# A two-layer transformer kernel on one core: column sums of the softmax weights by way of GpSimd in rows 1 to 6

## The reference, cut to what matters

```python
def _L1_attn_ref(x, Wq, bq, Wk, bk, Wv, bv, Wo, bo):
    B, S, _ = x.shape                     # D_MODEL, H, DK, DV = 128, 16, 64, 64
    q = (x @ Wq + bq).reshape(B, S, H, DK)
    k = x @ Wk + bk                       # one key head for all 16 query heads
    v = x @ Wv + bv
    scores = jnp.einsum('bshd,btd->bhst', q, k) / np.sqrt(DK)
    w = jax.nn.softmax(scores, axis=-1)
    out = jnp.einsum('bhst,btd->bshd', w, v).reshape(B, S, H * DV)
    return out @ Wo + bo
```

## Time and profile before

| | |
|---|---|
| median of 3 runs | 1322.18 us (1320.48 to 1323.92) |
| the profiled execution's own time | 1316.21 us |
| its span, first to last instruction | 1314.5 us |
| TensorE busy / weight loads | 1221.6 / 724.0 us |
| VectorE (DVE) busy | 957.3 us |
| ScalarE (ACT) busy | 680.7 us |
| GpSimd (POOL) busy | 256.2 us |

### The profile page before, as it was taken

How to read it: one execution, slowest core, us unless ns; L and a number is a source line. 1 busy time by engine, 2 the same in 40 slices (tenths; PEclk the granted TensorE clock), 3 DMA queues, 4 the chain that set the end, 5 groups by cost and what they waited for, 6 DMA issues and landing times.

```text
span 1314.5 us, 21957 instructions
## 1 busy us (share of the span) xinstructions
PE 1221.6 (93%) x7185; PEld 724.0 (55%) x7185; DVE 957.3 (73%) x2332; ACT 680.7 (52%) x1252; POOL 256.2 (19%) x311
## 2 busy tenths in 40 slices
PE   5459989999999999999999999999999989998997
PEld 2335445555555555545554555465545468775743
DVE  6876788578857885788578857885787567785865
ACT  4036556544554455445544554455444467775731
POOL 2033222200120012001200120012000226262630
PEclk9559999999999999999999999999999999998999
DMA  3073667233422351334223413351333557474471
GB/s 80 0 193 86 213 195 222 64 75 84 137 57 74 81 143 54 74 87 121 70 74 88 140 51 75 82 144 51 77 85 71 165 181 243 152 240 145 136 220 55
DMA packets 100020, 150.59 MB, mean 115 GB/s; under 512 B 35341, under 2 KB 51277, under 8 KB 95941
## 3 DMA queue, kind: packets, MB, share of 16 engines
q1 hardware_dynamic: 85348, 116.59, 32.5%
q0 software_dynamic: 11344, 31.64, 7.6%
q10 hardware_dynamic: 3216, 0.97, 0.3%
HBM read 59.86 MB, written 38.68 MB: 75 GB/s over the span
## 4 chain that ended last, share of the span: by engine, by line
PE 54%; DVE 18%; issue 12%; POOL 9%; ACT 4%; DMA 2%; SPq 1%; ACTq 0%; POOLq 0%; DVEq 0%
PE bank L1500 13%; POOL y_rows L734 7%; PE bank L1472 7%; PE bank L1511 6%; PE bank L1426 5%; PE bank L1473 5%; DVE mneg L1060 4%; PE bank L1532 3%; PE bank L1344 2%; ACT wide L872 2%; PE bank L1390 2%; PE bank L1369 1%; PE bank L1379 1%; PE bank L1328 1%; PE bank L1396 1%
## 5 line engine op out<-in xcount | busy, mean ns | idle before, releaser
L872 ACT ACTIVATE wide<-bank 128x512 f32<-128x512 f32 x512 | 294.6, 598 | 315.0 <-PE bank L1473 314.6
L1060 DVE TENSOR_REDUCE mneg<-bank 128x1 f32<-128x512 f32 x512 | 328.9, 684 | 148.4 <-PE bank L1426 144.4
L1500 PE MATMUL bank<-wide,v_w 128*32 128x512 f32 x2048 | 246.2, 598 | 1.0 <-issue 1.0
L1472 PE MATMUL bank<-q_hh,k_hl 128*128 128x512 f32 x512 | 232.5, 454 | 15.6 <-ACT wide L872 11.9
L1473 PE MATMUL bank<-q_lm,k_h 65*128 65x512 f32 x512 | 203.0, 396 | 0.0
L1472 PEld LDWEIGHTS bank<-q_hh,k_hl 128*128 128x128 f32 x512 | 96.3, 188 | 137.2 <-issue 79.1
L665 POOL TENSOR_TENSOR rs<-rs,power 128x4 f32<-128x4 f32 x24 | 24.5, 1020 | 615.6 <-DVE rs L946 615.5
L1511 PE MATMUL bank<-wide,ones 128*32 128x512 f32 x992 | 129.1, 592 | 0.0
L734 POOL DMA_INDIRECT y_rows<-y_m,to_u x92 | 97.3, 1058 | 131.4 <-DVE y_m L1186 110.1
L1500 PEld LDWEIGHTS bank<-wide,v_w 128*32 128x32 f32 x2048 | 53.5, 109 | 120.9 <-issue 113.1
L1426 PE MATMUL bank<-k_a,q_x 128*128 128x512 f32 x256 | 106.1, 415 | 4.8 <-ACT hqt L792 2.6
(11 more groups left out here) (252 smaller groups left out, 1945.2 us busy)
## 6 DMA issues: line engine op xcount, KB each, us to landing
q_hh<-q_x SPq DMA_DIRECT2D x256, 128.0 KB
w_t<-w_rows SPq DMA_DIRECT2D x23, 1024.0 KB
x_rows<-part_h POOLq DMA_DIRECT2D x65, 258.0 KB, 5.4
q_lm<-q_rest SPq DMA_DIRECT2D x128, 128.0 KB
inv<-inverse_scratch SPq DMA_DIRECT2D x124, 128.0 KB, 2.9
w_rows<-w_t SPq DMA_DIRECT2D x8, 1024.0 KB, 5.1
x_m<-x_rows SPq DMA_DIRECT2D x23, 258.0 KB, 3.8
stage<-in_L_ffn_W SPq DMA_DIRECT2D x16, 256.0 KB, 4.8
```

The costliest lines, as they stand in the source:

```text
L872: act.activation(wide[:, st.g % WIDE, :], ps, ACT.Exp, scale=SCALE1).then_inc(wide_full, 1)
L1060: dve.tensor_reduce(mneg[:, pair % 2, col:col + 1], ps[:], X, ALU.max, negate=True).then_inc(free, 1)
L1472: pe.matmul(ps, k_hl[:, n, t], q_hh[:, gh % HEADS, :], start=True, stop=False)
L1500: pe.matmul(ps_out[0][rows, :], v_w[:, n, c, TILE * d:TILE * d + TILE], weights, start=(c == 0), stop=(c == TT - 1))
```

## The change

In rows 1 to 6 (`added(pair)`: pairs 8 to 55, 48 of 64), the weights of two key quarters of one head are added on GpSimd before they are summed over partitions:

- `halve`, at steps with k % 4 of 2 and 3: `halves[half, b] = wide[g - 2] + wide[g]`, in two instructions of 128x256. Four such steps a pair.
- `values` no longer issues its `ones` matmuls for these pairs. Once a pair, one step after its last `values` (s = 2 of the next pair), `sums_of` issues 4 `ones` matmuls, on the four column groups. It waits for the last `halve`. ScalarE's `sraw` copy moves one step later.
- ScalarE's exponential also waits for the `halve` that reads the buffer it overwrites; `halve` waits for the `sums_of` of the pair before.
- GpSimd now walks the steps: roots at k = 30, 42, 51, scatters at 1 to 20, zeros at 24 to 37, one DMA at a step.
- The maxima are turned at s = 4, behind the step's two matmuls for maxima, instead of at s = 5.
- Some cuts of `L0_DVE` move by a step or two, layer 0's scale and shift goes behind the third down projection, "rk" (the counts) goes from k = 56 to 57.
- Memory is rearranged: `part_l` lies over layer 0's weights, `stage` over two of the four expert weight buffers, and in row 0 the experts' split uses two weight buffers instead of four.

```diff
-    L0_DVE = [-14, -11, -11, -10, -7, -6, -4, -2, 0, 0, 9, 10, 13, 17, 18, 21, 25, 26, 29, 30, 30, 31, 32,
-              34, 35, 37, 38, 39, 40, 42, 43, 44, 44]
+    L0_DVE = [-14, -13, -11, -10, -7, -6, -4, -2, 0, 0, 9, 10, 13, 17, 18, 21, 25, 26, 29, 30, 30, 31, 32,
+              34, 35, 37, 39, 39, 41, 42, 42, 44, 44]
...
+    FIRST_HALVED, LAST_HALVED = H // 2, (NB - 1) * (H // 2)
+    ROOT_AT = [30, 42, 51]
+    SCATTER_AT = [[1, 4, 5, 8], [13, 16, 17, 20]]
+    LAST_SCATTER_AT = [[0, 0, 0, 0], [1, 1, 1, 1]]
+    ZERO_AT = [24, 25, 28, 29, 32, 33, 36, 37]
...
-        if s == TT + 1 and 0 <= here + 1 < total:
-            events.append(("mt", here + 1))
         if s % 2 == 0:
...
+        if s == TT and 0 <= here + 1 < total:
+            events.append(("mt", here + 1))
...
+            def halve(st):
+                half, b, pair = st.k % PAIR // TT, st.k % 2, pair_of(st)
+                if pair > FIRST_HALVED:
+                    pool.wait_ge(summed, pair - FIRST_HALVED)
+                pool.wait_ge(wide_full, st.g + 1)
+                for q in range(2):
+                    cols = slice(S // 2 * q, S // 2 * q + S // 2)
+                    last = pool.tensor_tensor(halves[:, half, b, cols], wide[:, (st.g - 2) % WIDE, cols],
+                                              wide[:, st.g % WIDE, cols], ALU.add)
+                last.then_inc(halved, 1)
...
                     if st.g >= WIDE:
                         act.wait_ge(second_done, st.g - WIDE + 1)
+                        if st.g - WIDE in add_of:
+                            act.wait_ge(halved, add_of[st.g - WIDE])
...
+            def sums_of(pair):
+                free_bank(("ps", pair))
+                pe.wait_ge(halved, add_of[last_step(2 * pair + 1)])
+                for half in range(2):
+                    for b in range(2):
+                        rows = slice(DK * b + TILE * half, DK * b + TILE * half + TILE)
+                        last = pe.matmul(ps_out[1][rows, :], ones[:], halves[:, half, b, :], start=True, stop=True)
+                last.then_inc(summed, 1)
...
+                        if added(pair):
+                            last.then_inc(second_done, 1)
+                if added(pair):
+                    return
...
                 if block_end(st) is not None:
                     values(block_end(st))
+                pair = pair_end(st, 1)
+                if pair is not None and added(pair):
+                    sums_of(pair)
```

More of the change, by code:

```diff
@@ L188, in direct, with added, pair_of, adds @@
         return pair >= (NB - 1) * (H // 2) + DIRECT
+    def added(pair):
+        return FIRST_HALVED <= pair < LAST_HALVED
+    def pair_of(st):
+        return st.r * (H // 2) + st.k // PAIR
+    def adds(st):
+        return st.kind == "o" and st.k % TT >= 2 and added(pair_of(st))
     def tile_end(st):
@@ L281, in two_layers @@
     ring = Ring(SMALL, small_order)
+    add_of, count = {}, 0
+    for st in steps:
+        if adds(st):
+            count += 1
+            add_of[st.g] = add_of[st.g - 2] = count
     out_place, out_uses = {}, [0] * OUTB
@@ L287, in two_layers @@
             pair = st.r * (H // 2) + st.k // PAIR
-            names = [(("pv", pair), 0), (("ps", pair), 1)]
+            names = [(("pv", pair), 0)] + ([] if added(pair) else [(("ps", pair), 1)])
+        elif st.kind == "o" and st.k % PAIR == PAIR - 1 and added(pair_of(st)):
+            names = [(("ps", pair_of(st)), 1)]
         elif st.kind == "ye" and st.m == 0:
@@ L357, in two_layers @@
         part_h = sb("part_h", [P, PARTS, S], F32R)
[L358 to L361, removed]
+        halves = sb("halves", [P, 2, 2, S])
         def xq_of(n):
@@ L684, in _, with zero, scatter @@
                     .then_inc(split_l, 1)
[L687 to L696, removed]
+            def zero(n, e):
+                pool.dma_start(x_rows[ZONE * e + S * n:ZONE * e + S * (n + 1), :].rearrange("(p i) c -> p (i c)", p=P),
+                               zeros).then_inc(zeroed[n % 2], 16)
+            def scatter(n, b, i):
+                if i == 0:
                     if n or b:
@@ L715, in _ @@
[L715 to L735, removed]
+            pool.wait_ge(filled_up, 1)
+            pool.dma_start(x_rows[E * ZONE:, :].rearrange("(p i) c -> p (i c)", p=P), zeros).then_inc(zeroed[0], 16)
@@ new lines, in _ @@
+            for n in range(2):
+                for e in range(E):
+                    zero(n, e)
+            root()
+            for st in steps:
+                if st.kind == "o":
+                    if st.k in (ROOT_AT if st.r < NB - 2 else ROOT_AT[0:2] if st.r == NB - 2 else ()):
+                        root()
+                    if adds(st):
+                        halve(st)
+                    if st.r == 0 and st.k in SPLIT_STEPS:
+                        split_rest(SPLIT_STEPS.index(st.k))
+                    for b, at_ in enumerate(SCATTER_AT if st.r < NB - 1 else LAST_SCATTER_AT):
+                        for i in range(TT):
+                            if st.k == at_[i]:
+                                scatter(st.r, b, i)
+                    if st.k in ZERO_AT and st.r + 2 < NB:
+                        zero(st.r + 2, ZERO_AT.index(st.k))
+                if st.g is not None:
+                    here, i = divmod(st.g - 3, TT)
+                    if here - 2 in tile_of:
+                        scatter_y(tile_of[here - 2], i)
@@ L899, in _ @@
                 pair = pair_end(st, 1)
-                if pair is not None and not direct(pair):
+                if pair is not None and not direct(pair) and not added(pair):
                     act.wait_ge(second_done, last_step(2 * pair + 1) + 1)
+                    act.wait_ge(sums_stored[pair % 2], 16 * (pair // 2))
+                    act.activation(sraw[:, pair % 2, :], ps_out[1][:], ACT.Identity).then_inc(out_free[1], 1)
+                pair = pair_end(st, 2)
+                if pair is not None and added(pair):
+                    act.wait_ge(summed, pair + 1 - FIRST_HALVED)
                     act.wait_ge(sums_stored[pair % 2], 16 * (pair // 2))
@@ L1487, in values @@
                 if half == 0:
-                    for name in (("pv", pair), ("ps", pair)):
-                        b, uses = out_place[name]
-                        if uses:
-                            pe.wait_ge(out_free[b], uses)
+                    free_bank(("pv", pair))
+                    if not added(pair):
+                        free_bank(("ps", pair))
                     if st.k == TT - 1:
```

66 lines of the change are left out of this document (42 added, 24 removed).

## The result

| | before | after |
|---|---|---|
| median | 1321.33 us (1317.47 to 1323.92, 4 runs) | 1339.88 us (1338.04 to 1340.34, 4 runs) |
| ratio, 95% interval | | 1.0136 [1.0116, 1.0156] |
| span of the profiled execution | 1314.5 us | 1338.6 us |
| TensorE / VectorE / GpSimd busy | 1221.6 / 957.3 / 256.2 us | 1211.6 / 1010.7 / 542.6 us |

The forecast was 1302 and faster. The kernel became 18.6 us slower, beyond the range's upper end of 1326.

A forecast was written before the change was run, and what follows sets the result against it. TensorE was taken to bound the rows, VectorE second. The terms -25.5 (ones less the lone group), -9 (stalls) and +15 (VectorE's delays) gave -19.5 us, so 1302 us, range 1284 to 1326.

The forecast's parts named there:

- Ones removed: TensorE, 48 pairs: 8 `ones` matmuls become 4, saving 0.86 us a pair, 41.3 us in all.
- price of the lone group: TensorE: `sums_of` alone between full-array matmuls adds a change of array shape, 0.33 us a pair, 15.8 us in all.
- filled stalls: TensorE's waits around s = 2 to 4: `sums_of` fills them, gaining 1.5 us a row, 9 us in all.
- Rival D: The `ones` don't run side by side, or the saving isn't real: 1344 us, chance 0.03.
- GpSimd's lateness, 0: Waits for `halve` by `sums_of` and the exponential, and `halve`'s for `sums_of`: GpSimd about on time, costed at 0.
- the sentence on the roots: GpSimd's roots come first in their step, while VectorE writes the variance; GpSimd waits less than a step, costed at 0.
- VectorE's delays, +15: VectorE waits behind GpSimd's adds, 10 us a row; 2.5 us a row reaches TensorE, 1.3 in pair 4, 15 in all.
- Rival B: VectorE becomes the bound in pairs 4, 6 and 7, getting 30 us a row more: 1347 us, chance 0.09.
- One of my own signs of being wrong: TensorE's waits for VectorE or for `halved` exceed 4 us a row.
- Moved steps, 0: Turned maxima, `sraw`, scatters, zeros and counts at new steps: enough cover or free GpSimd time, nothing gained or lost.
- Row 0, "stays": Row 0 keeps its length; two weight buffers leave some 14 us against a store's 5.1 us, costed at 0.
- Row 7, "stays": Row 7, which has no halved sums, keeps its length: no change in time.

The follow-up runs named there:

- e6: The changed kernel without GpSimd's adds and with the counts back at k = 56: 1330.69 us, ratio 1.0022 to the kernel before.
- e10: e4 with each `halve`'s adds replaced by three GpSimd fills of 128x512 that read nothing from SBUF: 1292.63 us, ratio 0.9798.
- e4: The changed kernel with the counts back at k = 56 and VectorE's first slot cut at 57: 1324.10 us, ratio 1.0011.
- e1: The changed kernel without any add on GpSimd, the moved steps and new memory layout alone: 1335.58 us, ratio 1.0095.
- e5: The changed kernel with adds only in pairs 0, 1, 2, 3 and 5, row 0's zeros late, counts back: 1339.31 us, ratio 1.0079.
- e7: e6 with row 0's zeros late and four weight buffers for row 0's split: 1325.26 us, ratio 0.9979.
- e8: e5 with four weight buffers for row 0's split instead of two: 1338.19 us, ratio 1.0073.

## Why the prediction was wrong, step by step

A chain of kernels splits the result into the terms of the sum (differences of ratios, times 1321 us; each kernel differs from the next in one thing):

| step | what differs | predicted | measured |
|---|---|---|---|
| before to e6 | moves, counts not among them | 0 | +2.9 |
| e6 to e10 | ones halved, nothing reads SBUF | -34.5 | -29.6 |
| e10 to e4 | the adds read SBUF | +15 | +28.1 |
| e4 to after | counts at 57 | 0 | +16.5 |
| sum | | -19.5 | +18 |

e6, e10 and e4 ran on three different chips. By the spans of the profiled executions the first two steps are +11.6 and -36.9 instead of +2.9 and -29.6 and the others +33.2 and +16.2. The row lengths are the better measure of a term where no half clock falls: rows 1 to 5 of one trace agree to 0.1 us in the kernel before and in e6, and to 0.7 in e10. In e4, with half clocks, they run from 130.2 to 132.7.

*Ones removed, price of the lone group, filled stalls: right.* They were 41.3 - 15.8 + 9 = 34.5 us, 5.75 a row; the rows show 131.6 - 126.1 = 5.5, and the forecast lies between the two readings of the step. The 0.33 us a pair for the extra change of shape held to 0.01. Rival D is out.

*GpSimd's lateness, 0: nearly right.* The add is 768 ns, and TensorE waited for no `halve`. But the sentence on the roots ("GpSimd waits there for less than a step") was the one that mattered. It asked what the root does to the adds and not what the pent-up adds do to VectorE behind the root.

*VectorE's delays, +15: this term was mis-sized, though its first half was right.* I gave VectorE 10 us more a row. It got 9.6, and 53.4 in the whole kernel, within the 50 to 70 stated; the adds' own share is 7.8 a row (106.51 in e4, 98.70 in e10). What failed is the transfer: I took it to be spread over pairs, 1.3 us in pair 4 as long as its own adds are there. The delays come in a cluster instead. Four instructions that VectorE runs back to back (three of 0.16 us and `on`), all on the way to a bank that TensorE needs, met four half adds: 2.0 us in one place, and TensorE's ring of four banks passed nearly all of them on (18.12 against 16.31 us in pair 4), with the half clock behind it in five of six rows. The row takes up 4.1 us (126.11 to 130.20 in row 3; 5.1 on the mean of rows 1 to 6), where I had 2.5. Counting by chance (3 of 8) was no guide, since one event, the root, starts both sides. Rival B had the place and a wrong price: the VectorE time it assumed was three times what came, and it was still not needed for a loss. One of my own signs of being wrong was met: TensorE's waits for VectorE sum to 6.5 us in row 3 of the kernel after (2.9 + 2.8 + 0.3 + 0.3 + 0.2), where I had named 4.

The Trainium skill, "SBUF — State Buffer", Who interferes with whom, says that a VectorE instruction with two SBUF inputs contends with a GpSimd one that reads SBUF and not with one that only writes it. Here: 1009.5 us of VectorE with adds, 961.8 with fills. The page gives no price in time lost on another engine, and there is none to give apart from the place where it falls.

*Moved steps, 0: the largest miss.* The counts at k = 57 push VectorE's slot cut (58) behind a cut of the quantiser and two maxima (634.13 to 637 us above). In pair 7 TensorE then waits in order for `slot`: 1.5 us without adds (e1), 2.9 with them. Without adds the late counts are worth 9.6 us (e1 to e6, on two chips; rows 1 to 5 show 1.1 us of it each), with them 16.5, so the two aggravate each other: the wait grows, and half clocks follow it (pair 7 of row 1: 25.95 us, against 21.13 in e4). I had asked of "rk" only whether GpSimd has time for what follows, and not what on VectorE lies between its old and its new place, and who is queued behind.

*Row 0, "stays": +10.1.* I argued from stores of 5.1 us and two buffers, and so from the wrong wait; e5, e7 and e8 show no cost of the buffers beyond the scatter. Of the 10.1 us, 1.2 are pair 7 with its late counts. For the rest the loads were short of cover, with four steps ahead: late zeros give up to 3.9 us back, two steps more of lead 12.2. Which of the moves used up the cover that they had before isn't isolated; e1 says only that it is not the adds.

*Row 7, "stays": +4.7, and the cause stays open.* Its pair 0 goes from 15.29 to 20.86 us with the halved sums of row 6's last pairs, and not without them (14.21 in e1, 14.50 in e5). Reading SBUF isn't needed for it (21.21 with fills, e10). The row's length is another matter: it is 295.5 to 299.7 us in all the kernels after the change, and e1, without an add, has 299.3.

*The wait of the earlier trace rows gone*: right, the light pairs went from 13.45 to 12.32 us.

## What to carry to other kernels

When work is put on GpSimd beside VectorE, don't price it as an average: find the event that starts both (here the root), and put no reading GpSimd instruction behind it while VectorE runs a short chain that TensorE's next bank hangs on. A step moved by one place is costed by what lies between the two places on each engine that it touches, and by who waits in order behind it, however small the step is. Where an in-order engine takes a wait for a load, the lead of that load is part of every edit that shifts anything before it: two steps of lead were worth 12 us here.

## What the runs showed of the hardware

- A stall can cost more than its length. After stalls of TensorE of 2.8 to 5.0 us the granted clock stood at 0.50 for 3.4 us (pair 4) or 6.8 us (row 0) in many cases, not in all; the kernel before, whose longest wait in a middle row is 0.4 us and in row 0 1.7, shows none in rows 0 to 6. In pair 4 that was 1.1 us on top of 1.8 (18.12 against 19.20).
- Fills of 128x512 by GpSimd, 304 us of them, left VectorE's busy time at 961.8 us, against 957.3 before the change. Adds of 286.5 us cost it 47.7 us more.
- The form matters as much as the amount: 192 adds of 1327 ns hurt more than 384 of 770 (1.0169 against 1.0011), though they take 33 us less.
